# A state-space layer's chunk loop: both state products from high and low parts, and the state's update behind the projection to B and C

## The chip, the cores and the metric

The kernel runs on one core of a Trainium2 chip. The time is that of the device, in microseconds: the median of several executions. Beside it stands one profiled execution, from which every row here is taken.

## What is computed

The program is two transformer-like layers (a state-space mixer and three other parts, each with a residual and a layer norm). The change touches only the mixer, for 4 batches of 512 tokens of width 512. After an input projection, a short convolution and a SiLU (an earlier phase, which leaves x and z in DRAM), this is computed for each chunk, with 16 heads of 64 and a state of 128:

```python
proj = x_branch @ x_proj_w.T                     # X (1024), dt (16), B (128), C (128)
dt = softplus(dt @ dt_proj_w.T + dt_proj_b);  A = -exp(A_log)
X_scaled, A_scaled = X * dt[..., None], A * dt
Y_diag = einsum('bclgn,bcsgn,bghcls,bcsghp->bclghp', C, B, L, X)       # within a chunk
states = einsum('bclgn,bghcl,bclghp->bcghpn', B, decay_states, X)      # what a chunk adds to the state
Y_off  = einsum('bclgn,bcghpn,bghcl->bclghp', C, states, state_decay_out)  # from the state before
Y = (Y_diag + Y_off) + X * D
Y = Y * silu(z)
x = layernorm(x + Y @ out_proj_w.T)
```

The two state products are the third and the second einsum: C with the state, and B with the decayed X.

## The kernel before

`ssd_phase` holds the mixer behind the input projection. It works on 16 chunks of 128 tokens, four to a batch, and all weights stay in SBUF. Each of the five engines has its own program, written out by hand, and `chunks` calls its `step` once for each chunk; semaphores alone order one engine against another. An engine takes its instructions in the order of the code, and where one waits, all behind it wait.

Most matmuls are `product` (L86 to L88): each operand is split into a high part, rounded to fp32r (ScalarE copies), and a low part, the difference (a subtraction on VectorE or GpSimd), and three fp32r matmuls are summed. The two state products aren't: they are plain float32 matmuls on `state` and `xdec`.

A step g on **TensorE**: `y_off`, C by the state, into banks 0 and 1 of `pd` (L704); the product in the chunk, `mix` by `xs` (L712, 16 heads); the state's update, B by `xdec`, into `pa` and `pb` (L720); `bc_proj`, the projection of chunk g+1 to dt, B and C, into `pc`; the transposes of y (L732); `turn_bc`, the transposes of B and C (L664, L665); the projection to X (`x_part`, 48 matmuls in 16 parts), in which `cb_product` (C by B, L671), `a_sums` (L679, L681) and `exponents` (L692) are interleaved at fixed places; the output projection into `pc`.

**VectorE** in a step: the residual's sum for chunk g-1; y from `y_off` by its decay (L916); y plus X D (L920); the layer norm's statistics (L336, L339); y plus the product in the chunk (L925); the state's two halves (L931); the normalisation of chunk g-1 (L910); `dt_in` (L818 to L820); the gate `g_f` (L941); `dt_chain`, fourteen small operations of which each waits for the one before (L825 to L836, the five L831 among them); the masked CB (L842); the rows of the exponents; `xs` (L862); `mix` (L870).

**ScalarE**: `bc_copy`, `dt_exp`, `turned_copy` (L562, on which `cb_product` waits), `g_hi` (L636), and then the copies and exponentials of the decay. **GpSimd**: the state's decay (L537), the inverse deviation, `g_lo` (L543), X D (L522) and `xdec` (L528). **SP** issues the loads and stores: the residual's rows into `res`, x for chunk g+2, the store of `x1` from `rr`, z for g+1.

In the phase's setup the weights are split as well (`x_weights`, `wb_hi`, `wb_lo`), partly in memory that the loop uses later.

Of the kernel before, what the change touches and what calls it, by code (L numbers as in the profile page):

```python
# [90 lines left out]
def in_proj(nc, t, ident, pre, x0, wdt, per_head):  # L91
    with ExitStack() as ctx:
# [34 lines left out]
        def _(sp):  # L127
# [230 lines left out]
def ssd_phase(nc, t, ident, pre, x0, wdt, per_head):  # L358
    with ExitStack() as ctx:
        k = Kit(nc, ctx, "ssd")  # L360
        BC = NH + 2 * NS
# [3 lines left out]
        wb_hi, wb_lo = (k.sb(n, [P, IT, ROW], F32R) for n in ("wb_hi", "wb_lo"))  # L365
# [4 lines left out]
        res = k.sb("res", [P, DM])  # L370
# [15 lines left out]
        dtw = wdt[:, DI:DI + NH]  # L386
# [21 lines left out]
        xs, xd, y, g_f = (pre[:, 2 * HP + i * DI:2 * HP + (i + 1) * DI].rearrange("p (h d) -> p h d", h=h)  # L408
                          for i, h in enumerate((NH, NH, NH, IT)))
# [26 lines left out]
        s_sd, s_sa = k.sem("state_decayed"), k.sem("state_half_added")  # L436
        s_yT, s_g, s_ghi, s_glo = k.sem("y_transposed"), k.sem("gated"), k.sem("g_hi_ready"), k.sem("g_lo_ready")
# [57 lines left out]
        def _(pool):  # L495
# [12 lines left out]
            pool.wait_ge(s_const, 7)  # L508

# [45 lines left out]

# [2182 lines left out]
```

## Time and profile before

| | |
|---|---|
| time, median of 3 | 2403.33 us (2400.88 to 2404.07) |
| profiled execution | 2397.72 us, span 2396.0 us |
| TensorE | 2291.3 us busy, 96% of the span |
| VectorE | 1581.2 us, 66% |
| ScalarE | 849.5 us, 35% |
| GpSimd | 734.1 us, 31% |
| granted TensorE clock, mean | 0.981 |
| this phase, setup and loop | about 211 to 712 us |
| granted clock, 244 to 275 us (first chunk) | 0.83 |
| granted clock, 275 to 665 us | 1.00 |
| a DMA's issue to landing, x and z chunks and rows | 2.6 to 4.2 us (median by kind) |

The profiled execution is 5.6 us faster than the median of the timed ones. A busy share is an average over phases with different limits; what counts for a change in one phase is which engine is busy through there, and what the others' rows show beside it. TensorE's rows are modelled at their ends, since matmuls are pipelined: the distance from start to start says more than a row's length. A float32 matmul stands in the trace as two records.

### The profile page before, as it was taken

The numbers are of one execution on the slowest core, as the hardware profiler recorded it, in microseconds if no ns is written. First come the engines' busy times: TensorE is split into PE (matmuls) and PEld (weight loads), VectorE is DVE, ScalarE is ACT, GpSimd is POOL, SyncE is SP. The second block draws the span as 40 slices with busy tenths as digits, with TensorE's granted clock in tenths as the row PEclk, the third lists the DMA queues.
The fourth block names the chain that finished last, engine by engine and source line by source line (L and its number), as shares of the span: only waits on it lengthen the run. The fifth ranks groups of instructions, "written<-read, shape, count | busy, mean of one in ns | idle before, by whom it ended". The sixth has DMA issues, their size and how long they took to land.

```text
span 2396.0 us, 30727 instructions
## 1 busy us (share of the span) xinstructions
PE 2291.3 (96%) x10684; PEld 1862.0 (78%) x10684; DVE 1581.2 (66%) x2362; ACT 849.5 (35%) x1376; POOL 734.1 (31%) x538
## 2 busy tenths in 40 slices
PE   8997999999988999999999899999999999999997
PEld 6786788888866888887887688777778778888885
DVE  5556677777755956576354766667677886666665
ACT  5444222222224322232222344333344444444441
POOL 0002333333331222243121433233233543333331
PEclk9998999999998999999999999999999999999999
DMA  5645222222205001000000211222101121111110
GB/s 202 221 149 162 62 71 70 70 70 70 70 31 194 18 18 36 5 18 18 1 1 1 79 53 53 79 79 80 53 27 53 53 88 53 53 53 53 53 35 36
DMA packets 91013, 155.37 MB, mean 65 GB/s; under 512 B 6289, under 2 KB 55441, under 8 KB 84257
## 3 DMA queue, kind: packets, MB, share of 16 engines
q1 hardware_dynamic: 90912, 154.07, 19.1%
q8 instruction: 59, 0.97, 0.2%
q14 instruction: 42, 0.34, 0.0%
HBM read 114.20 MB, written 39.85 MB: 64 GB/s over the span
## 4 chain that ended last, share of the span: by engine, by line
PE 59%; DVE 6%; issue 2%; ACT 1%; POOL 1%; DMA 1%; SPq 0%; POOLq 0%; DVEq 0%; ACTq 0%
PE attn_pvk L972 4%; PE attn_pvk L974 4%; PE attn_pvk L973 4%; PE attn_pq L972 2%; PE attn_pq L973 2%; PE attn_pq L974 2%; PE attn_po L972 2%; PE attn_po L973 2%; PE attn_po L974 2%; PE attn_pv L972 2%; PE attn_pv L973 2%; PE attn_pv L974 2%; PE attn_pv L86 2%; PE attn_pv L88 2%; PE attn_pv L87 2%
## 5 line engine op out<-in xcount | busy, mean ns | idle before, releaser
L2357 DVE TENSOR_TENSOR moe_a_lo<-moe_up_raw,moe_a_hi 128x512 fp32r<-128x512 f32 x192 | 182.8, 968 | 154.9 <-ACT moe_a_hi L1820 154.8
L1702 POOL TENSOR_TENSOR moe_h_lo<-moe_c_t,moe_h_hi 128x512 fp32r<-128x512 f32 x96 | 128.5, 1339 | 354.9 <-ACT moe_h_hi L1820 354.9
L972 PE MATMUL attn_pvk<-moe_b_hi,moe_a_hi 128*128 128x512 f32 x512 | 200.5, 392 | 14.0 <-ACT moe_c_last L1946 6.0
L974 PE MATMUL attn_pvk<-moe_b_hi,moe_a_lo 128*128 128x512 f32 x512 | 199.4, 389 | 0.0
L973 PE MATMUL attn_pvk<-moe_b_lo,moe_a_hi 128*128 128x512 f32 x512 | 199.3, 389 | 0.0
L1820 ACT ACTIVATE moe_c_t<-attn_pvk 128x512 f32<-128x512 f32 x192 | 113.2, 596 | 185.5 <-PE attn_pvk L974 183.8
L1097 POOL TENSOR_TENSOR ffn_h_lo<-ffn_h_f,ffn_h_hi 128x512 fp32r<-128x512 f32 x64 | 89.9, 1404 | 266.0 <-ACT ffn_h_hi L1150 266.0
L1293 DVE SCALAR_TENSOR_TENSOR acc<-attn_pvk,ffn_wts,acc 128x512 f32<-128x512 f32 x128 | 91.2, 749 | 89.0 <-PE attn_pvk L88 88.7
L1872 ACT ACTIVATE moe_c_t<-moe_c_t 128x512 f32<-128x512 f32 x96 | 60.4, 629 | 241.7 <-DVE moe_c_t L2429 241.7
L1820 ACT ACTIVATE moe_a_hi<-moe_up_raw 128x512 fp32r<-128x512 f32 x192 | 116.0, 624 | 56.4 <-POOL moe_up_raw L1672 56.4
L972 PEld LDWEIGHTS attn_pvk<-moe_b_hi,moe_a_hi 128*128 128x128 f32 x512 | 96.1, 188 | 37.9 <-issue 11.3
L312 DVE SCALAR_TENSOR_TENSOR in_conv<-in_acc,in_cw,in_conv 128x511 f32<-128x511 f32 (+2 forms) x96 | 71.8, 748 | 75.4 <-ACT in_conv L258 73.2
L2389 DVE SCALAR_TENSOR_TENSOR acc<-attn_pv,moe_wts,acc 128x512 f32<-128x512 f32 x123 | 91.8, 746 | 42.3 <-PE attn_pv L974 40.4
L2429 DVE TENSOR_TENSOR moe_c_t<-moe_c_t,attn_po 128x512 f32<-128x512 f32 x128 | 86.3, 684 | 41.8 <-ACT moe_c_t L1820 35.9
L2389 DVE SCALAR_TENSOR_TENSOR acc<-attn_pq,moe_wts,acc 128x512 f32<-128x512 f32 x133 | 99.1, 745 | 22.3 <-PE attn_pq L974 19.3
L86 PE MATMUL in_acc<-in_x_hi,in_w_hi 128*128 (+1 forms) x256 | 101.7, 397 | 12.3 <-issue 6.4
L974 PEld LDWEIGHTS attn_pvk<-moe_b_hi,moe_a_lo 128*128 128x128 f32 x512 | 96.1, 188 | 20.2
L973 PEld LDWEIGHTS attn_pvk<-moe_b_lo,moe_a_hi 128*128 128x128 f32 x512 | 96.1, 188 | 19.4
L1672 POOL TENSOR_TENSOR moe_up_raw<-moe_up_raw 128x512 f32<-128x512 f32 x32 | 52.3, 1634 | 188.6 <-DVE moe_a_lo L2357 188.5
L972 PE MATMUL attn_pq<-moe_dn_hi,moe_h_hi 128*128 128x512 f32 x266 | 106.3, 399 | 1.1 <-DVE acc L2389 1.0
L972 PE MATMUL attn_po<-moe_b_hi,moe_a_hi 128*128 128x512 f32 x256 | 100.8, 394 | 4.4 <-DVE moe_c_t L2429 4.4
L973 PE MATMUL attn_pq<-moe_dn_lo,moe_h_hi 128*128 128x512 f32 x266 | 104.2, 392 | 0.0
(491 smaller groups left out, 6509.5 us busy)
## 6 DMA issues: line engine op xcount, KB each, us to landing
moe_up_raw<-in_e_up SPq DMA_DIRECT2D x28, 1024.0 KB, 5.6
moe_dn_raw<-in_e_dn SPq DMA_DIRECT2D x28, 512.0 KB, 3.5
xh<-in_out_hi SPq DMA_DIRECT2D x32, 256.0 KB, 2.6
zs<-in_out_z SPq DMA_DIRECT2D x32, 256.0 KB, 3.2
xl<-in_out_lo SPq DMA_DIRECT2D x32, 256.0 KB, 3.4
ssd_z_raw<-zs SPq DMA_DIRECT2D x16, 512.0 KB, 3.8
in_w_raw<-in_in_w SPq DMA_DIRECT2D x4, 1024.0 KB, 7.3
x<-xh SPq DMA_DIRECT2D x8, 512.0 KB, 4.2
```

The source lines that it names most:

```text
L86: pe.matmul(out, lh, rh, start=first, stop=False)
L312: nc.vector.scalar_tensor_tensor(out=conv[:, j % 2, d:SEQ], in0=acc[:, 2 * j % 4, 0:SEQ - d], scalar=cw[:, j, TAPS - 1 - d:TAPS - d], in1= ...
L972: pe.matmul(out, lh, rh, start=first, stop=False, skip_group_check=True)
L973: pe.matmul(out, lh, rl, start=False, stop=False, skip_group_check=True)
L974: return pe.matmul(out, ll, rh, start=False, stop=True, skip_group_check=True)
L1097: nc.gpsimd.tensor_tensor(h_lo[:, f], h_f[:, f % 2], raw(h_hi[:, f]), ALU.subtract).then_inc(s_hlo, 1)
L1293: stt(out=acc[:, ch], in0=pd[c], scalar=wts[:, ch, bass.ds(F * u + f, 1)], in1=acc[:, ch], op0=ALU.mult, op1=ALU.add).then_inc(s_acc, 1)
L1702: tt(h_lo[:, m, tok], src, raw(h_hi[:, m, tok]), ALU.subtract).then_inc(s_hlo, 1)
L1820: copy = lambda out, src: nc.scalar.activation(out, src, ACT.Copy)
L2357: tt_(a_lo[q][:], src, raw(a_hi[q][:]), ALU.subtract).then_inc(s_alo, 1)
L2389: stt(out=acc[:, ch], in0=bank, scalar=wts[:, ch, w] if isinstance(w, slice) else wts[:, ch, bass.ds(w, 1)], in1=acc[:, ch], op0=ALU.mult, ...
L2429: tt_(c_t[tile][:, i], c_t[tile][:, i], bank(i), ALU.add).then_inc(sem, 1)
```

## The change

What it does, in `ssd_phase`:

- Both state products go through `product`. For that `state`, B, C (transposed) and `xdec` each get a high part on ScalarE (`st_hi`, `b_hi`, `ct_hi`, `xdec_hi`) and a low part on GpSimd (`st_lo`, `b_lo`, `ct_lo`, `xdec_lo`).
- On TensorE the state's update stands behind `bc_proj`, no longer ahead of it.
- The residual is loaded into `rr`, the place of the result, once the store of `x1` from there has landed; `res` is gone.
- `g_f` has memory of its own and `g_lo` takes its place when it is done; `xdec` and its parts lie in memory of the earlier phase. The small weights of dt are loaded to 16 of 128 partitions of a wider buffer.

```diff
@@ GpSimd
+            pool.wait_ge(s_sthi, 1)
+            nc.gpsimd.tensor_tensor(st_lo[:], state[:], raw(st_hi[:]), ALU.subtract).then_inc(s_stlo, 1)
...
+            def parts(c):
+                pool.wait_ge(s_bhi, c + 1)
+                nc.gpsimd.tensor_tensor(b_lo[:], bcd[:, NH:NH + NS], raw(b_hi[:]), ALU.subtract).then_inc(s_blo, 1)
+                pool.wait_ge(s_cthi, c + 1)
+                nc.gpsimd.tensor_tensor(ct_lo[:], bct[:, NS:2 * NS], raw(ct_hi[:]), ALU.subtract).then_inc(s_ctlo, 1)
...
             def step(g, slot, turn, first, left):
                 if left:
...
+                    pool.wait_ge(s_stlo, g + 1)
                     nc.gpsimd.tensor_tensor(state[:], state[:], ek[:].unsqueeze(2).broadcast_to([P, NH, HD]),
                                             ALU.mult).then_inc(s_sd, 1)
+                    pool.wait_ge(s_xdhi, g + 1)
+                    nc.gpsimd.tensor_tensor(xdec_lo[:], xdec[:], raw(xdec_hi[:]), ALU.subtract).then_inc(s_xdlo, 1)
                 if not first:
                     inverse_deviation(nc, pool, mv[:], rstd[:], const[:], s_mv, s_eps, s_rstd, g)
                 if left:
+                    pool.wait_ge(s_sthi, g + 2)
+                    nc.gpsimd.tensor_tensor(st_lo[:], state[:], raw(st_hi[:]), ALU.subtract).then_inc(s_stlo, 1)
+                    parts(g + 1)
                     pool.wait_ge(s_ghi, g + 1)
                     nc.gpsimd.tensor_tensor(g_lo[:], g_f[:], raw(g_hi[:]), ALU.subtract).then_inc(s_glo, 1)
@@ ScalarE
+            def b_high(c, first=False):
+                act.wait_ge(s_bc, c + 1)
+                if not first:
+                    act.wait_ge(s_st, c)
+                nc.scalar.activation(b_hi[:], bcd[:, NH:NH + NS], ACT.Copy).then_inc(s_bhi, 1)
+            def state_high(c):
+                act.wait_ge(s_sa, 2 * c + 2)
+                nc.scalar.activation(st_hi[:], state[:], ACT.Copy).then_inc(s_sthi, 1)
...
             def step(g, slot, turn, first, left):
                 if left:
+                    decayed_high(g)
                     bc_copy(g + 1)
                     dt_exp(g + 1)
+                    b_high(g + 1)
                     turned_copy(g + 1)
+                    state_high(g)
                 act.wait_ge(s_g, g + 1)
...
                 if left:
+                    c_high(g + 1)
                     x_copy(g + 1, 0)
@@ TensorE
-                if first:
-                    pe.wait_ge(s_const, 7)
-                else:
-                    pe.wait_ge(s_sa, 2 * g)
+                pe.wait_ge(s_stlo, g + 1)
                 pe.wait_ge(s_rel, g + 1)
+                pe.wait_ge(s_ctlo, g + 1)
                 for i in range(2):
-                    ins = pe.matmul(pd[:, i], bct[:, NS:2 * NS],
-                                    state[:, i * half:(i + 1) * half].rearrange("p h d -> p (h d)"),
-                                    start=True, stop=True)
+                    part = lambda v: v[:, i * half:(i + 1) * half].rearrange("p h d -> p (h d)")
+                    ins = product(pe, pd[:, i], (ct_hi[:], ct_lo[:]), (part(st_hi), part(st_lo)))
                 ins.then_inc(s_yoff, 1)
...
                 if left:
-                    pe.wait_ge(s_xdec, g + 1)
-                    pe.wait_ge(s_xc, 2 * g + 2)
-                    for i, bank in enumerate((pa, pb)):
-                        ins = pe.matmul(bank[:], bcd[:, NH:NH + NS],
-                                        xdec[:, i * half:(i + 1) * half].rearrange("p h d -> p (h d)"),
-                                        start=True, stop=True)
-                    ins.then_inc(s_st, 1)
-
...
                     bc_proj(slot)
+
+                    pe.wait_ge(s_blo, g + 1)
+                    pe.wait_ge(s_xdlo, g + 1)
+                    pe.wait_ge(s_xc, 2 * g + 2)
+                    for i, bank in enumerate((pa, pb)):
+                        part = lambda v: v[:, i * half:(i + 1) * half].rearrange("p h d -> p (h d)")
+                        ins = product(pe, bank[:], (b_hi[:], b_lo[:]), (part(xdec_hi), part(xdec_lo)))
+                    ins.then_inc(s_st, 1)
@@ SP
             def step(g, slot, turn, first, left):
-                if not first:
-                    sp.wait_ge(s_rr, g)
-                sp.dma_start(res[:], t["x_rows"][bass.ds(g * P, P), :]).then_inc(s_lr, 16)
...
                     sp.dma_start(t["x1"][bass.ds(g * P - P, P), :], rr[:]).then_inc(s_out, 16)
+                    sp.wait_ge(s_out, 16 * g)
+                sp.dma_start(rr[:], t["x_rows"][bass.ds(g * P, P), :]).then_inc(s_lr, 16)
```

On ScalarE, in the loop's step from `bc_copy` to the first half of X, this stood before (L554 is `bc_copy`, L558 `dt_exp`, L562 `turned_copy`):

```order
L554 ACTIVATE ssd_bcd<-ssd_pc 128x272
L558 ACTIVATE ssd_u<-ssd_na 128x16
L562 ACTIVATE ssd_bct<-ssd_psm 128x256
L636 ACTIVATE ssd_g_hi<-pre 128x1024
L569 ACTIVATE ssd_xf<-ssd_pa 128x512
```

and this stands now (L580, L602, L608 are the same three; L594, L586, L598, L590 the four new high parts):

```order
L594 ACTIVATE ssd_xdec_hi<-ssd_xdec 128x1024
L580 ACTIVATE ssd_bcd<-ssd_pc 128x272
L602 ACTIVATE ssd_u<-ssd_na 128x16
L586 ACTIVATE ssd_b_hi<-ssd_bcd 128x128
L608 ACTIVATE ssd_bct<-ssd_psm 128x256
L598 ACTIVATE ssd_st_hi<-ssd_state 128x1024
L689 ACTIVATE ssd_g_hi<-ssd_g_f 128x1024
L590 ACTIVATE ssd_ct_hi<-ssd_bct 128x128
L615 ACTIVATE ssd_xf<-ssd_pa 128x512
```

Between `dt_exp` and `turned_copy` there is now the high part of B, and the high part of the state is ahead of `g_hi`.

On GpSimd, in the same step from the state's decay on, this stood before:

```order
L537 TENSOR_TENSOR ssd_state<-ssd_state,ssd_ek 128x1024
L345 TENSOR_TENSOR ssd_rstd<-ssd_mv,ssd_const 128x1
L347 TENSOR_TENSOR ssd_rstd<-ssd_rstd,ssd_const 128x1
L543 TENSOR_TENSOR ssd_g_lo<-pre,ssd_g_hi 128x1024
```

and this now:

```order
L555 TENSOR_TENSOR ssd_state<-ssd_state,ssd_ek 128x1024
L558 TENSOR_TENSOR ssd_xdec_lo<-ssd_xdec,ssd_xdec_hi 128x1024
L345 TENSOR_TENSOR ssd_rstd<-ssd_mv,ssd_const 128x1
L347 TENSOR_TENSOR ssd_rstd<-ssd_rstd,ssd_const 128x1
L563 TENSOR_TENSOR ssd_st_lo<-ssd_state,ssd_st_hi 128x1024
L544 TENSOR_TENSOR ssd_b_lo<-ssd_bcd,ssd_b_hi 128x128
L546 TENSOR_TENSOR ssd_ct_lo<-ssd_bct,ssd_ct_hi 128x128
L566 TENSOR_TENSOR ssd_g_lo<-ssd_g_f,ssd_g_hi 128x1024
```

Four subtractions are new: that of the decayed X ahead of the inverse deviation, and those of the state, B and C ahead of `g_lo`.

On TensorE, at the end of the projection to B and C of a step (the rows ahead of these are the last of `bc_proj`):

```order
 L88 MATMUL ssd_pc<-ssd_wb_hi,ssd_x 128x272
-L732 MATMUL ssd_pd<-ident,pre 128x128 x8
-L664 MATMUL ssd_psm<-ident,ssd_bcd 128x128
-L665 MATMUL ssd_psm<-ident,ssd_bcd 128x128
+L86 MATMUL ssd_pa<-ssd_xdec_hi,ssd_b_hi 128x512
+L87 MATMUL ssd_pa<-ssd_xdec_lo,ssd_b_hi 128x512
+L88 MATMUL ssd_pa<-ssd_xdec_hi,ssd_b_lo 128x512
+L86 MATMUL ssd_pb<-ssd_xdec_hi,ssd_b_hi 128x512
+L87 MATMUL ssd_pb<-ssd_xdec_lo,ssd_b_hi 128x512
+L88 MATMUL ssd_pb<-ssd_xdec_hi,ssd_b_lo 128x512
+L783 MATMUL ssd_pd<-ident,pre 128x128 x8
+L718 MATMUL ssd_psm<-ident,ssd_bcd 128x128
```

The six matmuls of the state's update stand between the projection and the transposes of y (L732, now L783), where before there was nothing; ahead of the projection their two float32 matmuls are gone.

## Rows read from the trace of the kernel before

**Rows 1.** Busy time by stretch, the middle of the phase (PEclk: granted clock).

```profile
core 0: us, PE busy (x) PEld busy (x) DVE busy (x) ACT busy (x) POOL busy (x), PEclk, DMA share, GB/s
455.00:485.00 30.00, 30.00 (x164) 24.42 (x163) 21.66 (x36) 8.13 (x12) 12.43 (x7) 1.00 0.24 70
```

**Rows 2.** Timeline of one step, TensorE: start us, us, then the instruction.

```profile
458.68 1.88 PE L704 MATMUL ssd_pd<-ssd_state,ssd_bct 128*128 128x512 f32 x4
460.40 3.68 PE L712 MATMUL ssd_pd<-pre 128*128 128x64 f32 x32
...
465.69 0.19 PEld L87 LDWEIGHTS ssd_pc<-ssd_wb_lo,x 128*128 128x128 f32 x1 [0.24 <-issue]
...
468.73 1.03 PE L732 MATMUL ssd_pd<-ident,pre 128*128 128x128 f32 x8
...
471.20 0.38 PE L671 MATMUL ssd_psm<-ssd_bct 128*128 128x128 f32 x2
...
477.60 0.38 PE L679 MATMUL ssd_psm<-ssd_tri,ssd_a_rep 128*128 128x128 f32 x2
...
488.16 1.88 PE L704 MATMUL ssd_pd<-ssd_state,ssd_bct 128*128 128x512 f32 x4
```

**Rows 3.** Timeline of the same step, VectorE.

```profile
456.63 3.33 DVE L870 TENSOR_TENSOR pre<-pre,ssd_cb_m 128x2048 f32<-128x2048 f32 x1 [0.58 <-ACT pre L596]
...
460.60 1.22 DVE L916 TENSOR_TENSOR pre<-ssd_pd,ssd_ed 128x1024 f32<-128x1024 f32 x1
461.86 2.81 DVE L920 TENSOR_TENSOR pre<-pre 128x1024 f32<-128x1024 f32 x1
464.59 0.68 DVE L336 BATCH_NORM_STATS2 ssd_stats<-ssd_rr 128x6 f32<-128x512 f32 x1
...
465.47 1.22 DVE L925 TENSOR_TENSOR pre<-pre,ssd_pd 128x1024 f32<-128x1024 f32 x1
466.61 0.75 DVE L931 SCALAR_TENSOR_TENSOR ssd_state<-ssd_pa,ssd_keep,ssd_state 128x512 f32<-128x512 f32 x1
...
467.93 0.54 DVE L910 TENSOR_SCALAR ssd_rr<-ssd_rr,ssd_mv,ssd_rstd 128x512 f32<-128x512 f32 x1
469.36 0.18 DVE L818 TENSOR_TENSOR ssd_v<-ssd_bcd,heads 128x16 f32<-128x16 f32 x1 [0.89 <-ACT ssd_bcd L554]
...
469.96 1.23 DVE L941 TENSOR_TENSOR pre<-ssd_pd,ssd_z_raw 128x1024 f32<-128x1024 f32 x1
...
472.22 3.10 DVE L831 SCALAR_TENSOR_TENSOR ssd_s<-ssd_s,ssd_q 128x16 f32<-128x16 f32 x5
...
475.99 0.28 DVE L842 TENSOR_TENSOR ssd_cb_m<-ssd_psm,ssd_tri 128x128 f32<-128x128 f32 x1
```

**Rows 4.** Timeline of the same step, ScalarE.

```profile
469.99 0.22 ACT L558 ACTIVATE ssd_u<-ssd_na 128x16 f32<-128x16 f32 x1 [0.66 <-DVE ssd_na L820]
470.11 0.36 ACT L562 ACTIVATE ssd_bct<-ssd_psm 128x256 f32<-128x256 f32 x1
471.30 1.06 ACT L636 ACTIVATE ssd_g_hi<-pre 128x1024 fp32r<-128x1024 f32 x1 [0.82 <-DVE pre L941]
```

**Rows 5.** Timeline of the same step, GpSimd.

```profile
457.78 3.95 POOL L528 TENSOR_TENSOR ssd_xdec<-pre,ssd_ed 128x1024 f32<-128x1024 f32 x1
461.69 1.90 POOL L537 TENSOR_TENSOR ssd_state<-ssd_state,ssd_ek 128x1024 f32<-128x1024 f32 x1
...
472.44 2.43 POOL L543 TENSOR_TENSOR ssd_g_lo<-pre,ssd_g_hi 128x1024 fp32r<-128x1024 f32 x1 [5.98 <-ACT ssd_g_hi L636]
```

**Rows 6.** Timeline of the setup, VectorE.

```profile
213.48 2.29 DVE L875 TENSOR_TENSOR ssd_wb_lo<-pre,ssd_wb_hi 128x2048 fp32r<-128x2048 f32 x1 [7.58 <-ACT ssd_wb_hi L603]
...
225.83 1.01 DVE L831 SCALAR_TENSOR_TENSOR ssd_s<-ssd_s,ssd_q 128x16 f32<-128x16 f32 x5
...
235.77 1.99 DVE L847 TENSOR_SCALAR ssd_d_cur<-ssd_c_hi,ssd_row_mask 128x128 f32<-128x128 f32 x1 [2.42 <-ACT ssd_c_hi L575]
```

**Rows 7.** Busy time by stretch in a phase of the experts.

```profile
1879.00:1887.50 8.50, 3.80 (x16) 2.55 (x15) 7.52 (x6) 5.13 (x8) 7.17 (x3) 1.00 0.00 0
1887.60:1890.90 3.30, 3.30 (x9) 2.61 (x8) 3.30 (x3) 3.05 (x5) 3.30 (x3) 0.50 0.00 0
```

More of the change, by code:

```diff
@@ L360, in ssd_phase @@
         k = Kit(nc, ctx, "ssd")
+        start = nc.sbuf_base
         BC = NH + 2 * NS
@@ L373, in ssd_phase @@
         xf = k.sb("xf", [P, NH, HD])
-        xdec = k.sb("xdec", [P, NH, HD])
+        xdec, xdec_lo = (nc.alloc_sbuf_tensor_at(f"ssd_{n}", [P, NH, HD], dt, offset=start - 4 * (4 * NH + 4 * DI))
+                         for n, dt in (("xdec", F32), ("xdec_lo", F32R)))
+        xdec_hi = nc.alloc_sbuf_tensor_at("ssd_xdec_hi", [P, NH, HD], F32R, offset=start - 4 * (4 * NH + DI))
         state = k.sb("state", [P, NH, HD])
-        g_hi, g_lo = k.sb("g_hi", [P, IT, P], F32R), k.sb("g_lo", [P, IT, P], F32R)
+        st_hi, st_lo = k.sb("st_hi", [P, NH, HD], F32R), k.sb("st_lo", [P, NH, HD], F32R)
+        b_hi, b_lo = k.sb("b_hi", [P, NS], F32R), k.sb("b_lo", [P, NS], F32R)
+        ct_hi, ct_lo = k.sb("ct_hi", [P, NS], F32R), k.sb("ct_lo", [P, NS], F32R)
+        g_hi, g_f = k.sb("g_hi", [P, IT, P], F32R), k.sb("g_f", [P, IT, P])
+        g_lo = nc.alloc_sbuf_tensor_at("ssd_g_lo", [P, IT, P], F32R, offset=nc.sbuf_base - 4 * DI)
         rr = k.sb("rr", [P, DM])
@@ L544, in step @@
                     skip_and_decay(g + 1)
+            parts(0)
             skip_and_decay(0, True)
@@ L561, in turned_copy @@
                 act.wait_ge(s_t2, c + 1)
+                if not isinstance(c, int) or c:
+                    act.wait_ge(s_ctlo, c)
                 nc.scalar.activation(bct[:], BCT, ACT.Copy).then_inc(s_bct, 1)
@@ L604, in _ @@
             x_weights(0)
+            act.wait_ge(s_const, 7)
+            nc.scalar.activation(st_hi[:], state[:], ACT.Copy).then_inc(s_sthi, 1)
             act.wait_ge(s_wdt, 1)
@@ L613, in _ @@
             x_weights(5)
+            b_high(0, True)
             turned_copy(0)
+            c_high(0)
             for i in (6, 7):
@@ L765, in _ @@
             for kt in range(IT):
-                ins = pe.matmul(WDT[:, kt * NH:(kt + 1) * NH], wdt[:, bass.ts(kt, P)], dtw, start=True, stop=True)
+                ins = pe.matmul(WDT[:, kt * NH:(kt + 1) * NH], wdt[0:NH, bass.ts(kt, P)], dtw, start=True, stop=True)
             ins.then_inc(s_wdt, 1)
@@ L895, in _, with residual_sum @@
             mixed(0)
-            def residual_sum(g, first=False):
-                if not first:
-                    dve.wait_ge(s_out, 16 * g)
+            def residual_sum(g):
                 dve.wait_ge(s_op, g + 1)
                 dve.wait_ge(s_lr, 16 * (g + 1))
-                tt(rr[:], pc[:], res[:], ALU.add).then_inc(s_rr, 1)
+                tt(rr[:], pc[:], rr[:], ALU.add).then_inc(s_rr, 1)
             def statistics(g):
@@ L913, in step @@
                 if not first:
-                    residual_sum(g - 1, isinstance(g, int) and g == 1)
+                    residual_sum(g - 1)
                 dve.wait_ge(s_yoff, g + 1)
@@ L951, in _ @@
             dve.wait_ge(s_ghi, NCH)
-            tt(g_lo[:], g_f, raw(g_hi[:]), ALU.subtract).then_inc(s_glo, 1)
+            tt(g_lo[:], g_f[:], raw(g_hi[:]), ALU.subtract).then_inc(s_glo, 1)
             residual_sum(NCH - 1)
```

29 lines of the change are left out of this document (20 added, 9 removed).

## The prediction

> **What bounds the kernel now.** I read the busy shares by stretch first. In the loop over chunks TensorE is busy for the whole of each stretch [rows 1]: this phase (about 244 to 700 us) is TensorE-bound, so what TensorE is spared there shortens the kernel, unless something new makes it wait. Then I read one step in order of time, engine by engine. On TensorE [rows 2] a step lasts 488.16 - 458.68 = 29.48 us, and nothing stands between its pieces. The reader is to see the reserve at two places. The product in the chunk starts at 460.40, and `mix`, which it reads, is ready at 456.63 + 3.33 = 459.96 [rows 3]: a reserve of 0.44. The sums of a start at 477.60, and what they wait for, the masked CB at the end of VectorE's dt chain, is over at 475.99 + 0.28 = 476.27: a reserve of 1.33.
>
> The third thing is that VectorE and GpSimd hold each other up. The five links L831 take 1.01 us in the setup, with GpSimd idle [rows 6], and 3.10 in the step, where GpSimd's `g_lo` (2.43) starts 0.2 behind them [rows 3, 5]: 2.09 lost. The addition L920 takes 2.81 from 461.86 beside GpSimd's 1.90 from 461.69; GpSimd's `xdec` takes 3.95, since it stands from 457.78 until `mix` is over at 459.96 and then needs about 1.9, as the state's decay does. Where one is running, the other waits for its end, and the one that waits comes next. L916, which reads PSUM, runs beside `xdec` and isn't held (1.22). The Trainium skill ("SBUF — State Buffer", "Who interferes with whom") has this as a rule: a VectorE instruction with two SBUF inputs and a GpSimd instruction that reads SBUF block one another fully. By that rule, and the trace agrees (2.09), the change's new GpSimd subtractions speak against it.
>
> **What the change saves.** 31 products of two float32 matmuls (16 from the state, 15 for it) become six of fp32r. The old ones take 460.40 - 458.68 = 1.72; one of fp32r of 512 columns takes (477.60 - 471.20 - 0.22) / 27 = 0.229, 27 of them standing between the CB product and the sums of a, and 0.22 for the CB product is my estimate from its two records. Six take 1.37, so 0.35 is saved on each product. The Trainium skill ("FP8 and Floating Point Precision", "TensorE Precision Notes") counts true FP32 as four passes; three single ones would save a quarter, 0.43, and 0.16 a step more than the rows give. The rows decide.
>
> **The step after the change**, in the trace's own times, from 458.68.
> 1. The product from the state is issued by 460.05. The product in the chunk waits for `mix`, 459.96, and some 0.15 behind it can start (between 0 and the 0.44 that lie between them now): 460.11 for 460.40. Saved: 0.29, not 0.35.
> 2. The projection's first matmul really begins when the second's weights are loaded, at 465.69 [rows 2]. So the product in the chunk takes 465.69 - 1.72 - 460.40 = 3.57, and B and C's projection, now next, 468.73 - 465.69 = 3.04: TensorE is at the state's update at 466.72.
> 3. That needs `xdec_lo`. `xdec` ends at 461.73, its high part (ScalarE, 1.06, else idle) at 462.8, the state's decay on GpSimd at 463.59. VectorE's L920, which waited, comes next and ends at 464.67; then `xdec_lo`, 2.4 like `g_lo`, ends at 467.0, and the product starts at 467.15. **TensorE waits 0.43.** It then spares the second 0.35 and is through at 468.52, its last result some 0.17 later. The covered part is thin: with `xdec_lo` at 1.9 there is no wait.
> 4. Now VectorE is late. Its two additions to the state began at 466.61, with `y` only; now at 468.74. They, the normalisation and `dt_in` are queued on one engine: 0.66 each for the first three (466.61 to 467.93 is two), less 0.2 for the shorter last one, and 0.60 from `dt_in` to the gate (469.36 to 469.96). The gate starts at 468.74 + 1.32 + 0.46 + 0.60 = 471.12, **1.16 later than now**.
> 5. Behind `dt_in` hangs ScalarE: `dt_exp` moves from 469.99 to 471.15, and `turned_copy` stands behind it and behind the new `b_high` (0.2 of issue; its neighbours of 16 and 256 columns take 0.22 and 0.36 [rows 4]). It ends at 471.81, and the CB product can start at 471.96. TensorE is there at 468.52 + (471.20 - 468.73) = 470.99. **TensorE waits 0.97.** Before, the projection's place gave this its cover; its move takes the cover away.
> 6. TensorE is at the sums of a at 471.96 + 6.40 = 478.36. Without any hold VectorE's chain would be over 6.31 - 2.09 = 4.22 behind the gate's start, at 475.34. But `state_high` (1.06) ends at 472.8, so `st_lo` (2.4) holds the chain from there to 475.2, about 2.2; `b_lo` and `ct_lo` (128 columns, about 0.4 each, an estimate from 2.43 for 1024 and 0.2 of start) cost some 0.5; and `g_lo` follows at 476.2, with 1.8 of chain left, and holds it 2.1 as today. The chain ends at 480.1, the sums start at 480.27. **TensorE waits 1.9.**
> 7. From there to the next step nothing is changed: 488.16 - 477.60 = 10.56.
>
> Sum of a step: -0.29 - 0.35 + 0.43 + 0.97 + 1.9 = +2.66. Steps 0 to 14 have the state's update: 15 x 2.66 = 40. The first, partly at a lower clock, I take like the others, for want of a better row; in the last, with no update, nothing is gained or lost above 0.3.
>
> **Setup.** `st_hi` and `st_lo` of the zero state are new. L875 ends at 215.77 [rows 6]; GpSimd's `st_lo` then goes first, 2.3 until 218.1, and VectorE's first low part of the X weights waits, with the small low part behind it for which TensorE's first projection stands idle. TensorE is then late by 2.3. That a VectorE instruction with one tensor from SBUF can be held too, L847 shows: 1.99 beside GpSimd, where L842 has 0.28 for as many elements [rows 3, 6].
>
> **At nothing:** the residual's load now waits for the store of `x1` to land, and the load of z is queued behind it on SP. The store goes out at about 471, the residual is needed at 489: 18 us cover it, and without cover it would cost the landing of two transfers in each step, some 6 us by the table's 2.6 to 4.2 for one. `g_hi` goes from 471.3 to 472.7, `g_lo` is over at 478.6 and needed at 485: covered.
>
> The profiled execution took 2397.7, so 2397.7 + 40 + 2.3 = 2440.0. The median shown is 5.6 above it, and I forecast for a median: 2445.6, say **2446**.
>
> **Prices with two ends.** A GpSimd subtraction may take 1.9, like the forms with a broadcast, not 2.4: then steps 3 and 6 lose 0.43 + 2 x 0.5, and the sum is 15 x 1.2 + 2 = 20: 2424. I take 2.4, the row of the same form. The statistics L336 come to stand beside `xdec_lo`. If they aren't held (as L916), nothing; if they are (as L847), `y` is ready 2.4 later at 469.1, the additions start 0.3 later and the step is 0.3 longer: 2451. I take nothing: they read one tensor. The small `b_lo` and `ct_lo`: 0 to 1.0 together, 2439 to 2453.
>
> **The rivals.**
> - *The clock falls* (16%). TensorE's waits of 0.97 and 1.9 could lower its granted clock from 2.4 to 1.2 GHz. In a phase of the experts a stretch with 4.7 of 8.5 us idle was followed by one granted 0.50 [rows 7]; a step has 3.3 idle of 32. If it falls in each step for 3.3 us, half of it, 1.65, is lost: 15 x 1.65 = 25, 2471; in a third of the steps, 2454.
> - *Only one long hold meets the chain, or the holds are shorter* (14%). The chain would have to be over before `g_lo`, that is before 476.2. Then step 6 costs nothing: 15 x 0.76 + 2.3 = 14, 2417; with both holds at 1.9, 2424.
> - *GpSimd's work holds nothing* (7%). Steps 3 and 6 fall away and step 5 has about 0.5: a step gets 0.1 shorter to 0.3 longer, and the kernel takes 2402 to 2408. L831's 3.10 for 1.01 speaks against it.
> - *Faster* (6%): one mechanism, that `turned_copy` isn't late. It decides at 470.84, 0.15 before TensorE is at the CB product. Were `dt_in` ready by 470.1 (the additions 1 us sooner) and the subtractions without holds, 0.64 a step would be kept: 15 x 0.64 = 10, 2394. Against it: on VectorE, ScalarE's copy hangs behind the additions by its order.
> - *As walked through* (57%): 2446, its own range 2436 to 2458.
>
> **How the numbers follow.** The range leaves out the faster case, the one without holds and the worst of the clock's: 2420 to 2470. A measurement can't tell less than about 0.2%, 4.8 us. Faster 5%, the same 7% (most of the case without holds), slower 88%.
>
> **What would show it.** TensorE idle before the CB product (about 1.0, on ScalarE) and before the sums of a (about 1.9, on VectorE's masked CB), 15 times each; about 0.4 before the state's update, on GpSimd; a step of 32.1; L831's group not at 3.10 but near 5.2; the product from the state in 1.37. Wrong would be: no idle time before the sums of a (then the holds don't add up), or a granted clock below 1.00 in the middle of the phase.

## The result and the profile after

The changed kernel takes 2462.12 us (median of 4, 2459.66 to 2462.54), the kernel before in the same comparison 2403.70 (2400.88 to 2404.47). The ratio is 1.0247, with an interval of 1.0232 to 1.0262: 58 us slower. I had forecast 2446, 43 us slower, with a range to 2470. The profiled execution took 2462.53 us, with a span of 2460.8. In the comparisons of the experiments the kernel before has medians of 2398.5 to 2400.0 (8 to 22 executions), so the 2403.7 of this one is at the high end, and the change may well cost 60 us or a little more; e1 and e9, which differ little from it, stand at 1.0266 and 1.0258.

The page's head and busy shares, of the kernel after:

```profile
span 2460.8 us, 31060 instructions
PE 2316.5 (94%) x10746; PEld 1888.3 (77%) x10746; DVE 1623.0 (66%) x2362; ACT 885.1 (36%) x1439; POOL 834.2 (34%) x601
```

TensorE is busy for 25 us more and the span is 65 longer: most of it is waiting, and part of the 25 is the same work at half the clock (below). The waits of TensorE by cause, kernel after, 200 to 800 us (waiting instruction, what it waited for, us in total, times, longest):

```profile
engine line waited for: us in total, times, longest us
PE ssd_psm L733 <- DVE ssd_a_rep L887: 24.3, 15, 1.6
...
PE ssd_psm L725 <- ACT ssd_bct L608: 9.7, 15, 0.7
...
PE ssd_pc L86 <- DVE ssd_wb_lo L929: 4.2, 1, 4.2
...
PE ssd_pa L86 <- POOL ssd_xdec_lo L558: 2.8, 12, 0.2
```

The reader is to see the three waits that the prediction placed: before the sums of a (L733), before the CB product (L725) and before the state's update (`ssd_pa`, L86). None was there in a step before [rows 2].

Then the phase by steps. Each stretch runs from one product from the state to the next, kernel after:

```profile
core 0: us, PE busy (x) PEld busy (x) DVE busy (x) ACT busy (x) POOL busy (x), PEclk, DMA share, GB/s
246.24:285.99 39.75, 34.35 (x165) 29.28 (x165) 22.55 (x32) 11.73 (x16) 19.66 (x10) 0.87 0.24 67
285.99:318.33 32.34, 29.82 (x165) 24.49 (x164) 23.83 (x36) 9.88 (x15) 18.36 (x11) 1.00 0.23 66
...
487.59:521.46 33.87, 31.34 (x165) 25.45 (x164) 23.80 (x36) 9.87 (x15) 18.34 (x11) 0.95 0.22 62
521.46:553.71 32.25, 29.69 (x165) 24.49 (x164) 23.82 (x36) 9.88 (x15) 18.38 (x11) 1.00 0.23 65
...
511.40:514.70 3.30, 3.30 (x12) 2.12 (x10) 1.17 (x3) 0.48 (x1) 0.00 (x0) 0.50 0.00 0
```

There are two kinds of step: 32.05 to 32.34 us at a granted clock of 1.00, and 33.65 to 33.95 at 0.95. Of the 14 steps behind the first, 3 are of the first kind and 11 of the second. The last row lies inside one of the second kind: 3.3 us granted 0.50, that is 1.2 of 2.4 GHz, with TensorE busy throughout. It comes 2.1 us behind the end of the wait before the sums of a (which start at 509.30 there). Of the rows shown for before, only the first chunk was below 1.00 in this phase.

The sum closes. Steps 0 to 14 take 754.90 - 246.24 = 508.66, for 450.57 before: +58.1. In it the first step has +1.7, the other fourteen 14 x (32.21 - 29.47) = +38.4, and eleven of them another 1.63 each, +17.9. Ahead of it stand 2.4: the first product from the state starts at 246.24, for 243.87. That is 2.9 from the setup (35.21 from the phase's first matmul, at 211.03, for 32.31 from 211.56), less 0.5 by which the phase began sooner. What comes behind the start of the last chunk's step takes 1705.9, for 1701.6, and over the profiles of this study's kernels between 1700.9 and 1706.4. Of the 4.3, 0.8 lie ahead of the next phase's first matmul (29.30 for 28.50). The rest lies in code that is the same in all of them, and isn't put down to the change.

One step at full clock, in order of time (start us, us, instruction, in brackets the idle time before it and what ended it). TensorE:

```profile
521.46 0.40 PE L86 MATMUL ssd_pd<-ssd_st_hi,ssd_ct_hi 128*128 128x512 f32 x1
...
522.90 3.76 PE L763 MATMUL ssd_pd<-pre 128*128 128x64 f32 x32
...
529.97 0.49 PE L86 MATMUL ssd_pa<-ssd_xdec_hi,ssd_b_hi 128*128 128x512 f32 x1 [0.24 <-POOL ssd_xdec_lo L558]
...
531.47 1.03 PE L783 MATMUL ssd_pd<-ident,pre 128*128 128x128 f32 x8
...
534.81 0.49 PE L725 MATMUL ssd_psm<-ssd_bct 128*128 128x128 f32 x2 [0.68 <-ACT ssd_bct L608]
...
543.08 0.46 PE L733 MATMUL ssd_psm<-ssd_tri,ssd_a_rep 128*128 128x128 f32 x2 [1.64 <-DVE ssd_a_rep L887]
...
553.71 0.40 PE L86 MATMUL ssd_pd<-ssd_st_hi,ssd_ct_hi 128*128 128x512 f32 x1
```

VectorE in the same step:

```profile
527.38 0.68 DVE L336 BATCH_NORM_STATS2 ssd_stats<-ssd_rr 128x6 f32<-128x512 f32 x1
...
531.67 0.75 DVE L980 SCALAR_TENSOR_TENSOR ssd_state<-ssd_pa,ssd_keep,ssd_state 128x512 f32<-128x512 f32 x1 [2.18 <-PE ssd_pb L88]
...
534.03 1.23 DVE L990 TENSOR_TENSOR ssd_g_f<-ssd_pd,ssd_z_raw 128x1024 f32<-128x1024 f32 x1
...
535.88 2.33 DVE L879 TENSOR_TENSOR ssd_q<-ssd_na 128x16 f32<-128x16 f32 x1
...
538.66 3.37 DVE L882 SCALAR_TENSOR_TENSOR ssd_s<-ssd_s,ssd_q 128x16 f32<-128x16 f32 x5
...
542.70 0.28 DVE L893 TENSOR_TENSOR ssd_cb_m<-ssd_psm,ssd_tri 128x128 f32<-128x128 f32 x1
```

ScalarE and GpSimd:

```profile
534.07 0.21 ACT L602 ACTIVATE ssd_u<-ssd_na 128x16 f32<-128x16 f32 x1 [3.90 <-DVE ssd_na L871]
534.19 0.29 ACT L586 ACTIVATE ssd_b_hi<-ssd_bcd 128x128 fp32r<-128x128 f32 x1
534.39 0.36 ACT L608 ACTIVATE ssd_bct<-ssd_psm 128x256 f32<-128x256 f32 x1
...
526.34 3.39 POOL L558 TENSOR_TENSOR ssd_xdec_lo<-ssd_xdec,ssd_xdec_hi 128x1024 fp32r<-128x1024 f32 x1
...
535.78 2.40 POOL L563 TENSOR_TENSOR ssd_st_lo<-ssd_state,ssd_st_hi 128x1024 fp32r<-128x1024 f32 x1 [5.27 <-ACT ssd_st_hi L598]
538.13 0.47 POOL L544 TENSOR_TENSOR ssd_b_lo<-ssd_bcd,ssd_b_hi 128x128 fp32r<-128x128 f32 x1
538.55 0.46 POOL L546 TENSOR_TENSOR ssd_ct_lo<-ssd_bct,ssd_ct_hi 128x128 fp32r<-128x128 f32 x1
538.97 2.40 POOL L566 TENSOR_TENSOR ssd_g_lo<-ssd_g_f,ssd_g_hi 128x1024 fp32r<-128x1024 f32 x1
```

The gate (L990) starts 12.57 us into the step, for 11.28 before [rows 3]: 1.29 later. One link of the dt chain (L879), of which its neighbours of that size take 0.17, stands at 2.33 until `st_lo` ends; the five links (L882) take 3.37 beside `b_lo`, `ct_lo` and `g_lo`, for 1.01 free [rows 6]. So the chain carries two long holds, where it carried one.

### The profile page after: what moved, and what is told of

Read it like the earlier page. It is cut to its first block, busy times and chain, and to the rows that moved or that the text cites. A ratio compares the mean times of both kernels' runs of the same rounds, so it can differ in the third digit from the quotient of the medians.

```text
span 2460.8 us, 31060 instructions
## 1 busy us (share of the span) xinstructions
PE 2316.5 (94%) x10746; PEld 1888.3 (77%) x10746; DVE 1623.0 (66%) x2362; ACT 885.1 (36%) x1439; POOL 834.2 (34%) x601
## 4 chain that ended last, share of the span: by engine, by line
PE 58%; DVE 6%; issue 2%; ACT 1%; POOL 1%; DMA 0%; SPq 0%; POOLq 0%; DVEq 0%; ACTq 0%
PE attn_pvk L1021 4%; PE attn_pvk L1022 4%; PE attn_pvk L1023 4%; PE attn_pq L1021 2%; PE attn_pq L1023 2%; PE attn_pq L1022 2%; PE attn_po L1021 2%; PE attn_pv L1021 2%; PE attn_po L1022 2%; PE attn_po L1023 2%; PE attn_pv L1022 2%; PE attn_pv L1023 2%; PE attn_pv L86 2%; PE attn_pv L88 2%; PE attn_pv L87 2%
## 5 line engine op out<-in xcount | busy, mean ns | idle before, releaser
L86 PE MATMUL in_acc<-in_x_hi,in_w_hi 128*128 (+1 forms) x256 | 101.7, 397 | 11.6 <-issue 5.7
L1023 PE MATMUL attn_pq<-moe_dn_hi,moe_h_lo 128*128 128x512 f32 x266 | 103.7, 390 | 0.0
```

What stands on the lines that cost most here:

```text
L86: pe.matmul(out, lh, rh, start=first, stop=False)
L1023: return pe.matmul(out, ll, rh, start=False, stop=True, skip_group_check=True)
```

## The experiments

Times are medians, ratios stand against the kernel before in the same comparison. Two theories went in. **A**: VectorE's dt chain, late by its start and held by GpSimd, sets the step, and the wait before the sums of a then lowers the clock. **B**: each wait adds on its own (the copy of the transposes, `xdec_lo`), or the extra work does.

### e1: the copy of the transposes first

```diff
@@ ScalarE, step
+                    turned_copy(g + 1)
                     dt_exp(g + 1)
                     b_high(g + 1)
-                    turned_copy(g + 1)
```

> The changed kernel with turned_copy ahead of dt_exp and b_high on ScalarE. Theory A (VectorE's chain sets the step, and TensorE's wait before the CB product only moves into the wait before the sums of a): the wait of 0.68 before the CB product is gone, the one before the sums of a grows from 1.63 to about 2.3, a step at full clock stays at 32.25, and the time stays within 2 us of 2462, or rises by up to 5 where the longer wait takes the clock down in more steps. Theory B (the two waits add up, as my prediction summed them): the wait before the sums stays at 1.63, a step takes 31.6, and the time is about 2452.

Measured: 2463.85, 1.0266 (1.0249 to 1.0283). TensorE's waits from 275 to 700 us, in this kernel:

```profile
PE ssd_psm L733 <- DVE ssd_a_rep L887: 32.3, 13, 2.6
```

The wait before the CB product is gone, and the one behind it has grown from 1.6 to 2.5 us. The steps stay at 32.0 to 32.2 and 33.6 to 33.9, again 3 and 11 of them. So, in this kernel, the two waits are one delay seen at two places: VectorE's chain decides when the sums start, and a wait of TensorE ahead of that costs nothing. Theory A holds, rival B doesn't: the time isn't 2452.

### e2: three subtractions behind the chain

```diff
@@ GpSimd, step
+                    pool.wait_ge(s_ghi, g + 1)
+                    nc.gpsimd.tensor_tensor(g_lo[:], g_f[:], raw(g_hi[:]), ALU.subtract).then_inc(s_glo, 1)
+                    pool.wait_ge(s_cbm, g + 2)
                     pool.wait_ge(s_sthi, g + 2)
                     nc.gpsimd.tensor_tensor(st_lo[:], ...
                     parts(g + 1)
-                    pool.wait_ge(s_ghi, g + 1)
-                    nc.gpsimd.tensor_tensor(g_lo[:], g_f[:], raw(g_hi[:]), ALU.subtract).then_inc(s_glo, 1)
```

> The changed kernel with st_lo, b_lo and ct_lo on GpSimd behind g_lo and behind the masked CB, so that of the long subtractions only g_lo meets VectorE's dt chain. Theory (GpSimd's subtractions hold the chain): the five L882 take about 3.1 as before the change, the q operation 0.17 and not 2.33, the wait before the sums of a is gone (1.63 of idle and some 0.2 of start), the wait of 0.68 before the CB product stays, a step takes about 30.4, the clock stays at 1.00, and the time is 2462 - 15 x 1.8 - 12 x 1.6 = 2416. Rival (the chain is late for another reason, its later start): the wait before the sums stays above 1 and the time above 2445. Rival on the clock (its falls have nothing to do with TensorE's waits): steps of 33.9 beside 32.3 are still there, less 1.8 each, and the time is about 2435.

Measured: 2415.62, 1.0061 (1.0044 to 1.0078). Steps 1 to 14 as one stretch, and the waits:

```profile
283.66:708.80 425.14, 412.70 (x2297) 343.95 (x2296) 297.35 (x491) 138.28 (x210) 257.55 (x141) 1.00 0.22 64
...
PE ssd_psm L726 <- ACT ssd_bct L609: 9.5, 14, 0.7
PE ssd_pa L86 <- POOL ssd_xdec_lo L558: 2.8, 12, 0.2
```

The wait before the sums is gone, and a step is 30.2 to 30.5. The same instructions run, only at another time: some 45 us (1.0061 for 1.0247) hung on the place of `st_lo`, `b_lo` and `ct_lo`, with what the clock gave back, since with the long wait its falls went too. The wait of 0.7 before the CB product stayed and costs, now that nothing behind it swallows it.

### e3: both

> Both of the two edits before it. Theory A: with the chain no longer held twice, the wait before the CB product is the one that sets the step, so turned_copy first now pays: no wait before the CB product, at most 0.2 before the sums of a, a step of 29.8, time about 2407. If the CB wait cost nothing here either: 2416.

Measured: 2408.47, 1.0038 (1.0024 to 1.0053), with steps of 29.6 to 30.1. A small hold is left, at the row of the exponents on VectorE, shown with GpSimd's row that holds it:

```profile
485.32 1.06 DVE L899 TENSOR_SCALAR ssd_d_cur<-ssd_c_hi,ssd_row_mask 128x128 f32<-128x128 f32 x1 [1.49 <-ACT ssd_c_hi L622]
...
483.92 2.38 POOL L566 TENSOR_TENSOR ssd_st_lo<-ssd_state,ssd_st_hi 128x1024 fp32r<-128x1024 f32 x1 [1.70 <-DVE ssd_cb_m L894]
```

### e4: matmuls of no use in the wait

Seven fp32r matmuls of 512 columns into a free bank stand ahead of the sums of a. Their result is overwritten.

```diff
@@ TensorE, step, ahead of a_sums
+                    for _ in range(7):
+                        pe.matmul(pc[:], xin[slot][:, 0, 0], wx_hi[:, 0, 0:512], start=True, stop=True)
```

> The changed kernel with seven extra fp32r matmuls of 512 columns into pc (whose content is no longer needed) ahead of the sums of a, in each step: TensorE works through its wait instead of standing idle. They add work, about 1.6 us a step, and nothing reads their result. Theory (the granted clock falls because of the idle time before the sums of a): all steps take 32.25 to 32.4, the clock stays at 1.00 between 290 and 750 us, and the time falls by 12 x 1.6 = 19 to about 2443, with more work done. Rival (the clock falls for another reason, or the longer steps aren't the clock's doing): the time stays at 2462 or rises.

Measured: 2442.94, 1.0177 (1.0161 to 1.0194). The seven, the sums of a right behind them, steps 1 to 14 as one stretch, and the wait before the CB product from 275 to 700 us:

```profile
532.38 1.75 PE L799 MATMUL ssd_pc<-ssd_wx_hi,ssd_x 128*128 128x512 f32 x7
534.17 0.46 PE L733 MATMUL ssd_psm<-ssd_tri,ssd_a_rep 128*128 128x128 f32 x2
...
286.59:738.06 451.47, 438.34 (x2396) 361.35 (x2394) 333.31 (x491) 138.25 (x210) 256.75 (x141) 1.00 0.21 61
...
PE ssd_psm L725 <- ACT ssd_bct L608: 8.8, 13, 0.7
```

TensorE does 1.75 us more in each step, and the kernel is faster than the change by 0.7%, some 17 us: the fourteen steps take 451.5 for 468.9. All are of the 32.1 to 32.3 kind. The wait of 0.7 before the CB product is still there. So the falls of the clock hang on the idle time before the sums, and they are worth what the rows say, 1.6 us each. This kernel is nearly what I had forecast, and it is the change without the clock.

### e5: the move alone

The kernel before, with its float32 state's update behind `bc_proj`; on ScalarE `bc_copy` waits for it (not shown in the cut).

```diff
@@ TensorE, step
+                    bc_proj(slot)
                     pe.wait_ge(s_xdec, g + 1)
                     ...
                     ins.then_inc(s_st, 1)
-                    bc_proj(slot)
```

> The kernel before, with one part of the change alone: the state's update (still float32) behind the projection to B and C, and bc_copy waiting for it. Theory (the move takes away the cover that the projection gave to VectorE's additions, the gate and turned_copy): the additions to the state start about 2.5 later than before, turned_copy ends 1.5 later, TensorE waits about 1.2 before the CB product and not before the sums of a, a step takes about 30.7, and the time is 2403.7 + 15 x 1.2 = 2422. Rival (the move is free, and only the subtractions cost): 2404.

Measured: 2411.15, 1.0049 (1.0035 to 1.0063), with steps of 30.2 to 30.4 and this wait of TensorE:

```profile
PE ssd_psm L673 <- ACT ssd_bct L564: 6.7, 14, 0.5
```

The move costs 12 us and saves nothing. I had expected 18. The copy ends 1.44 later, as I had it, but I had put 1.2 of that down as a wait; before the change the copy was over at 470.47 and read at 471.20 [rows 2, 4], so 0.7 of the delay was free.

### e6: the change without the move

The changed kernel, with the state's update back ahead of the projection, and `xdec_lo` as late as it is.

> The changed kernel with the state's update back ahead of the projection. It then waits for xdec_lo, which ends at 529.7 in the changed kernel's trace, while the product in the chunk is through at 526.5: TensorE waits about 3.1 there. Behind it everything on VectorE comes as in the changed kernel, and turned_copy is later still, since the projection follows. Theory: a step of 33 to 34.5, no wait before the CB product, less than 1.6 before the sums of a, and the time between 2465 and 2485: the move was right once the parts are there. Rival (the move is what costs): below 2450.

Measured: 2517.48, 1.0492 (1.0476 to 1.0508). The waits, one step, and two stretches in it:

```profile
PE ssd_pa L86 <- POOL ssd_xdec_lo L558: 35.8, 11, 3.3
PE ssd_psm L733 <- DVE ssd_a_rep L887: 13.7, 11, 1.3
...
510.97:548.57 37.60, 33.10 (x166) 27.60 (x165) 23.93 (x36) 9.87 (x15) 18.33 (x11) 0.86 0.19 56
...
517.30:524.00 6.70, 4.59 (x15) 4.04 (x16) 3.09 (x6) 0.00 (x0) 2.55 (x3) 0.50 0.00 0
537.80:541.10 3.30, 3.30 (x9) 2.62 (x8) 1.73 (x5) 0.49 (x1) 0.00 (x0) 0.50 0.00 0
```

The sign and the wait on `xdec_lo` came as expected, the size didn't: I had left out the clock, which falls in each step around the wait for `xdec_lo` (6.7 us, 4.59 of them busy) and behind the wait before the sums (3.3 us). By these rows half of 7.9 busy us is lost, and 37.6 less 3.9 is 33.7, an estimate within the 33 to 34.5 that I had expected. So the move is bad by itself and needed once the update has to wait for a low part.

### e7: the residual alone; e9: the product from the state plain again

e7 is the kernel before with only the residual's load moved to `rr`; e9 is the changed kernel with one edit:

```diff
@@ TensorE, step (e9)
-                    ins = product(pe, pd[:, i], (ct_hi[:], ct_lo[:]), (part(st_hi), part(st_lo)))
+                    ins = pe.matmul(pd[:, i], bct[:, NS:2 * NS], part(state), start=True, stop=True)
```

> The kernel before, with the residual loaded into the result's place alone. Both theories: nothing, within 0.2% of 2403.7, since the load has 15 us between the store's landing and its use. If the queue on SP mattered (the load of z waits behind it), a step would be longer and the time above 2410.

> The changed kernel with the product from the state as two float32 matmuls again (all parts are still made, and waited for). Theory: TensorE has waits behind it in each step, so the 0.35 it spared there is worth nothing in the changed kernel: the wait for xdec_lo shrinks from 0.24 to 0, the rest is as before, and the time stays within 3 us of 2462. Rival (TensorE's work counts in full): 16 x 0.35 = 5.6 more, 2468.

Measured: e7 2400.13, 1.0003 (0.9994 to 1.0012), nothing. e9 2461.24, 1.0258 (1.0244 to 1.0272), with the same two kinds of step as the change (9 of its 14 are long, in the profiled execution): under a chain on VectorE that sets the step, the 0.35 us of TensorE are worth nothing.

### e8: all subtractions out of VectorE's way; e10: and the zero state's parts by memset

e8 is e3 with `g_lo` behind the masked CB and the other three behind the last row of the exponents. e10 is e8 with zeroes written to `st_hi` and `st_lo` in the setup, without ScalarE's copy of the zero state and the subtraction.

```diff
@@ GpSimd (e8 against e3, step)
+                    pool.wait_ge(s_cbm, g + 2)
                     pool.wait_ge(s_ghi, g + 1)
                     nc.gpsimd.tensor_tensor(g_lo[:], ...
-                    pool.wait_ge(s_cbm, g + 2)
+                    pool.wait_ge(s_dr, g + 2)
                     pool.wait_ge(s_sthi, g + 2)
                     nc.gpsimd.tensor_tensor(st_lo[:], ...
@@ GpSimd (e10 against e8, setup)
+            nc.gpsimd.memset(raw(st_hi[:]), 0.0).then_inc(s_sthi, 1)
+            nc.gpsimd.memset(raw(st_lo[:]), 0.0).then_inc(s_stlo, 1)
-            nc.gpsimd.tensor_tensor(st_lo[:], state[:], raw(st_hi[:]), ALU.subtract).then_inc(s_stlo, 1)
```

> e3_both with g_lo on GpSimd behind the masked CB too, and st_lo, b_lo and ct_lo behind the rows of the exponents: no GpSimd subtraction meets VectorE's dt chain. Theory: the five L883 take 1.0, the chain is over 2 us ahead of the sums of a, TensorE waits only 0.2 for xdec_lo, a step takes 29.0 to 29.4 and the two products' saving shows at last; with the setup's 2.4 the time is 2397 (2394 to 2401), at or below the kernel before (2399.1 in the last runs). Rival (the late gate, not the holds, keeps a step near 30): 2406.

> e8_all_behind, and the parts of the zero state in the setup by two memsets on GpSimd and not by a copy and a subtraction. Theory (in the setup st_lo holds VectorE's first low part of the X weights, and a memset reads nothing from SBUF and holds nothing): the first L846 takes 1.2 and not 3.4, TensorE's first projection starts 2.3 sooner, and the time is 2.3 below that of e8_all_behind. Rival: a memset holds it as well, or the setup has slack there: no difference.

Measured: e8 2403.00, 1.0011 (1.0002 to 1.0020), steps of 29.2 to 29.5; e10 2400.39, 0.9998 (0.9989 to 1.0007). First e8 (the five links free again; the wait for `xdec_lo`; the first addition to the state and the start of X's first half), then e10's setup (the two memsets, VectorE's low part of B and C's weights beside them, and the low part that was held in the change):

```profile
475.86 1.01 DVE L884 SCALAR_TENSOR_TENSOR ssd_s<-ssd_s,ssd_q 128x16 f32<-128x16 f32 x5
...
469.45 0.49 PE L86 MATMUL ssd_pa<-ssd_xdec_hi,ssd_b_hi 128*128 128x512 f32 x1 [0.22 <-POOL ssd_xdec_lo L558]
...
471.24 0.75 DVE L982 SCALAR_TENSOR_TENSOR ssd_state<-ssd_pa,ssd_keep,ssd_state 128x512 f32<-128x512 f32 x1 [2.26 <-PE ssd_pb L88]
472.05 0.50 PE L86 MATMUL ssd_pa<-ssd_wx_hi,x 128*128 128x512 f32 x1
```

```profile
215.64 2.29 DVE L927 TENSOR_TENSOR ssd_wb_lo<-pre,ssd_wb_hi 128x2048 fp32r<-128x2048 f32 x1 [7.60 <-ACT ssd_wb_hi L652]
215.68 0.95 POOL L518 MEMSET ssd_st_hi<- 128x1024 f32 x1
...
216.57 0.95 POOL L519 MEMSET ssd_st_lo<- 128x1024 f32 x1
...
217.85 1.22 DVE L847 TENSOR_TENSOR ssd_wx_lo<-pre,ssd_wx_hi 128x1024 fp32r<-128x1024 f32 x1
```

With every hold on the chain gone, e8 was still 6 us above what I expected: a step is no shorter than before, although its cheaper state products should spare 0.7. The step that begins at 460.98 shows where it goes. The transposes of y start 9.95 us into it, for 10.05 before: the wait for `xdec_lo`, 0.4 by starts, eats most of what was spared. From there to the CB product it takes 2.61, for 2.47 [rows 2]. For that I have a reading from rows that e11 bears out but doesn't test by itself: X's first half goes into the bank from which the first addition to the state reads, and TensorE starts it (472.05) right when that addition ends (471.99). e10 gave its 2.6 us: the low part of X's weights takes 1.22, for 3.37 in the change, and the setup is 2.5 shorter in the profile (32.71 from the phase's first matmul, for e8's 35.20).

### e11: the transposes of y ahead of the update

e10 with the transposes of y ahead of the state's update, to cover the wait for `xdec_lo`.

> e10_zero_state with the transposes of y ahead of the state's update on TensorE, so that xdec_lo has 0.9 more time. Theory (the chain now has slack): the wait of 0.24 for xdec_lo (and some 0.1 of start) is gone, the additions to the state come 0.5 later and cost nothing, a step is 0.3 shorter, the time 4 us below e10_zero_state, 2391 to 2394. Rival (the later additions delay the gate and the chain sets the step again): 0 to 8 us above it.

Measured: 2409.00, 1.0035 (1.0023 to 1.0047). TensorE's waits:

```profile
PE ssd_pa L86 <- DVE ssd_state L982: 9.4, 14, 0.7
```

I was wrong. The wait for `xdec_lo` went, but the additions to the state came later, and X's first half waits 0.7 for its bank. That speaks for the reading under e8: behind the update there is no slack in that bank.

### e12: the product from the state alone

e10, but with the state's update as before: float32, and ahead of the projection. `b_hi`, `b_lo`, `xdec_hi` and `xdec_lo` fall away.

> One part alone, put where it holds nothing: only the product from the state comes from parts (st_lo and ct_lo on GpSimd behind the rows of the exponents, g_lo behind the masked CB, the zero state's parts by memsets), the state's update is float32 and ahead of the projection as before the change, with no parts of B and of the decayed X. Theory (the step is TensorE's again, and of the 0.35 spared 0.29 comes through, since mix then is what the product in the chunk waits for): no waits of TensorE, a step of 29.2, the time 15 x 0.27 = 4 us below the kernel before, 2396 beside 2400.0. Rival (mix, not TensorE, already sets the start of the product in the chunk): a step of 29.4 to 29.5 and no difference.

Measured: 2397.21, 0.9991 (0.9982 to 1.0000). Steps 1 to 14:

```profile
283.73:693.30 409.57, 409.57 (x2269) 339.72 (x2268) 267.06 (x491) 120.67 (x182) 205.12 (x113) 1.00 0.23 67
```

TensorE never waits, and a step is 29.25, 0.22 shorter than before in the profile: of the change, this is the part that pays. By its median it is the fastest version of the study, 1.3 us below the kernel before in its comparison, which is too little to be told from no change.

## Why the prediction was right in its steps and short in its sum

**The step.** Distances from its start, as walked and as measured at full clock: product in the chunk 1.43 and 1.44; end of `xdec_lo` 8.3 and 8.27; state's update 8.5 and 8.51; CB product 13.3 and 13.35; sums of a 21.6 and 21.62; next step 32.1 and 32.25. From its start to what follows, the product from the state takes 1.44 and the state's update 1.50 (its first matmul, behind a wait, takes 0.1 more), for 1.37 to 1.43 expected. The three idle times stand in the trace at 0.24, 0.68 and 1.64, for 0.43, 0.97 and 1.9: a row's modelled end lies up to 0.2 behind the next possible start, so by starts (529.44 to 529.97, with 0.13 from one matmul of that kind to the next) the first is 0.40.

**The holds.** `st_lo`, `b_lo`, `ct_lo` and `g_lo` take 2.40, 0.47, 0.46 and 2.40 on GpSimd, so 2.4 was the right end, not 1.9. The chain lost about 4.5 (2.33 + 3.37 for 0.17 + 1.01) where I had 4.8. I had put both long holds in L831's group at 5.2; one met the link ahead of it. The statistics L336, for which I had a price with two ends, stood beside `xdec_lo` and took 0.68: not held. The rule of the Trainium skill ("SBUF — State Buffer", "Who interferes with whom"), that an instruction of VectorE with two SBUF inputs and a GpSimd instruction that reads SBUF shut each other out, agrees with all the rows of this chain. What that costs here, e2 shows: some 45 us for the place of three subtractions, falls of the clock included.

**Setup, residual, products.** The term of 2.3 for the setup measured 2.2 (the wait before TensorE's first projection is 4.20, for 2.04 in the kernel before and in e10), the whole setup 2.9; residual 0 (e7). Of the saving of 0.35 on the product from the state, a step shows 0.22 in e12, where I had given it 0.29, and in the change it is buried (e9).

**What failed: the size of the clock's term.** The step that said 15 x 2.66 = 40, with the clock kept, was a case apart from the rival in which it falls. Both happened. The waits came as walked, and behind the one before the sums the clock fell in 11 of 14 steps, at 1.63 us each, for the 1.65 that the rival had from half of 3.3 us. So one of the two signs that I had named for being wrong came, a granted clock below 1.00 in the middle of the phase, and 2462 lies outside the 2436 to 2458 that I gave to the case as walked through; only the wide range, which took in most of the rival, holds it. The sum so corrected is 40 + 2.3 + 18 = 60, for 58.1 + 2.4 measured in the profile. On top of the profile before it would give 2458 without the 5.6 for the median, and 2464 with it. That the second is near 2462.1 is luck: the changed kernel's profile stands at its median, not 5.6 below, and the 4.3 us behind the phase, which I had at nothing, happen to make up for it. I had given the falling clock 16% because the only row at hand had 4.7 us of idle time ahead of a fall [rows 7]; 1.64 in one piece, with 0.68 some 7 us ahead of it, were enough here, and in e1 one piece of 2.5. e4 shows the link: fill the long piece, leave the short one, and the clock stays.

**A wrong reason in a right sum.** I added the wait before the CB product to that before the sums. e1 shows that they don't add: without the first, the second takes over its length. My step came out right because I had walked both on one time line. In e2, with the chain in time, the first wait does cost.

**The rivals that fell.** One hold only (2417) is what e2 makes (2415.6), with the order changed by hand. No holds (2402 to 2408) is e8 (2403.0); e3, at 2408.5, still has `g_lo` beside the chain. Faster at 2394 never came: e12, the best, has 2397.2 and doesn't move the update at all.

**Left open.** Why three of the fourteen steps keep the clock, with the same waits. Whether the bank, tested by itself, takes the last tenths in e8.

## What to carry to other kernels

When matmuls are made cheaper by high and low parts, the new subtractions are the change: price what they hold up on VectorE, and put them behind the chain of small operations that TensorE waits for, not beside it. A wait of TensorE that is a small part of a step (1.64 us of 32 here) can cost as much again by its clock, so add both in one case. Waits behind one another on one late chain are one delay: test which engine sets the step before curing the first.

## What the runs showed of the hardware that I had not expected

- An idle time of 1.64 us, beside a smaller one of 0.68, in a step of 32 was followed by 3.3 us at a granted clock of 0.50 in 11 of 14 steps; one of 0.7 with 0.2 ahead of it (e2) or of 0.5 (e5) by none. Work of no use in its place made the kernel 17 us faster (e4).
- Of VectorE's instructions with one tensor from SBUF, some are held and some aren't: L899 took 1.06 in e3, until `st_lo` ended, for 0.29 free, and L336 took its 0.68 beside `xdec_lo`.
- Two of GpSimd's memsets held nothing: both of 0.95, from 215.68 on, stood beside a subtraction of VectorE with two tensors from SBUF, which took 2.29 as without them [rows 6] (e10).
- A hold falls on one small operation as fully as on a large one: 2.33 for 0.17.
